# Attention of a graph layer: 24 visits of 53 targets instead of 20 of 63, scores as rows, the mask inside the maximum

## The reference

```python
x = x * rsqrt(mean(x^2) + EPS) * rms_w
x = x @ W_down
xl, xr = (x @ Wl).reshape(n, 4, 64), (x @ Wr).reshape(n, 4, 64)
msg = xl[src] + xr[dst]
act = where(msg > 0, msg, 0.2 * msg)
e = einsum('ehd,hd->eh', act, att)
m = segment_max(e, dst)
p = exp(e - m[dst])
alpha = p / (segment_sum(p, dst)[dst] + 1e-16)
out = segment_sum(alpha[..., None] * xl[src], dst)
out = out.reshape(n, 256) @ W_up
```

## Time and profile before

| | us |
|---|---|
| median of 3 timed runs | 1574.01 (1572.9 to 1575.59) |
| profiled execution: span from first to last instruction | 1688.0 |
| TensorE busy | 1587.7 (94%) |
| VectorE busy | 819.2 (49%) |
| ScalarE busy | 387.0 (23%) |
| GpSimd busy | 259.4 (15%) |
| mean granted TensorE clock | 0.941 of full |

### The profile page before, as it was taken

The page is one execution under the profiler, slowest core; times in us unless marked ns, Lnnn a source line. Parts: engine busy times, 40 slices in busy tenths (PEclk is TensorE's granted clock), DMA queues, the critical chain, the costliest instruction groups (busy, mean ns, idle before and its releaser), DMA issues.

```text
span 1688.0 us, 21080 instructions
## 1 busy us (share of the span) xinstructions
PE 1587.7 (94%) x8256; PEld 1360.5 (81%) x8256; DVE 819.2 (49%) x1262; ACT 387.0 (23%) x699; POOL 259.4 (15%) x306
## 2 busy tenths in 40 slices
...
GB/s 43 177 167 191 128 125 93 129 110 119 137 117 97 112 149 101 115 65 102 132 83 51 127 219 202 88 94 150 0 1 224 187 180 144 156 38 0 63 181 106
DMA packets 99519, 198.38 MB, mean 118 GB/s; under 512 B 24908, under 2 KB 58980, under 8 KB 99420
## 3 DMA queue, kind: packets, MB, share of 16 engines
...
q10 hardware_dynamic: 1482, 0.20, 0.1%
...
## 4 chain that ended last, share of the span: by engine, by line
PE 52%; DVE 1%; ACT 0%; issue 0%; POOL 0%; DVEq 0%; ACTq 0%
PE layers_y_ps L1755 33%; PE layers_y_ps L1776 16%; PE layers_turn_ps L1739 2%; PE layers_up_ps L1723 1%; PE layers_y_ps L1792 1%; DVE layers_w_lo L1912 0%; PE layers_turn_ps L1711 0%; ACT L312 0%; DVE layers_parts_lo L1923 0%; DVE layers_y L1956 0%; POOL out L1696 0%; ACT layers_parts_hi L1867 0%; ACT layers_w_hi L1850 0%; DVE layers_y L631 0%; DVE layers_y L2018 0%
## 5 line engine op out<-in xcount | busy, mean ns | idle before, releaser
L1171 POOL DMA_INDIRECT attention_got<-xl_d,attention_src x130 | 130.5, 1004 | 144.0 <-DVE attention_weighted L1400 101.9
L1213 PEld LDWEIGHTS attention_score_ps<-edges_att_pick,attention_bent 128*128 128x128 f32 x800 | 137.4, 242 | 9.3 <-issue 1.6
L1776 PE MATMUL layers_y_ps<-layers_parts_hi,layers_counts 128*128 128x512 f32 x464 | 143.6, 391 | 0.0
L1776 PE MATMUL layers_y_ps<-layers_parts_lo,layers_counts 128*128 128x512 f32 x464 | 143.3, 390 | 0.0
L1250 PE MATMUL attention_mix_ps<-attention_weighted,attention_hot 128*126 128x260 f32 x400 | 126.9, 439 | 17.0 <-issue 15.5
L1171 POOL DMA_INDIRECT attention_got<-xl_d,heads_first_src x70 | 73.6, 1052 | 353.0 <-issue 308.2
L1755 PE MATMUL layers_y_ps<-layers_w_hi,layers_parts_hi 128*128 128x512 f32 x400 | 125.9, 396 | 0.0
L1755 PE MATMUL layers_y_ps<-layers_w_lo,layers_parts_hi 128*128 128x512 f32 x400 | 123.6, 390 | 0.0
L1755 PE MATMUL layers_y_ps<-layers_w_hi,layers_parts_lo 128*128 128x512 f32 x400 | 123.6, 390 | 0.0
L1213 PE MATMUL attention_score_ps<-edges_att_pick,attention_bent 128*128 128x4 f32 x800 | 121.5, 275 | 1.7 <-issue 1.7
L1360 DVE TENSOR_REDUCE attention_pair_max<-attention_spread_ps 128x2 f32<-128x512 f32 x100 | 68.6, 687 | 95.2 <-PE attention_spread_ps L1219 51.4
(11 more groups left out here) (312 smaller groups left out, 3020.5 us busy)
## 6 DMA issues: line engine op xcount, KB each, us to landing
...
```

The lines of the kernel that those rows point to most:

```text
L1171: pool.indirect_dma_start(got[s][:, t, :], None, xl_d, bass.IndirectOffsetOnAxis(src[s][:, t:t + 1], 0))\
L1213: nc.tensor.matmul(score_ps[j % 2][:, 2 * q + u, :], bent[c][:, k * PAIR + u * P:k * PAIR + (u + 1) * P], g["att_pick"][:, k, :], start=(q ...
L1776: last = nc.tensor.matmul(y_ps[n % 2][:, a:a + HALF], counts[c % 2][:, k, :], part[k][:, a:a + HALF], start=(k == 0 and part is hi), stop= ...
```

## The change

A visit now has 53 targets (24 visits) and a window of 1024 edges, 8 tiles in two quads of 4. The unit of work is 512 edges by one half `k` of the features, four units a visit (`UNITS`), so that a message unit is four transposes and one product of 512 columns. The two copies of the targets now stand on partitions 0 to 52 and 64 to 116 (`PART` = 64).

Scores are now made once, as rows: `att_rows` are the weights, `bent` in f32 is the moving side of 512 columns, and the four units of a visit add up in one PSUM bank `row_ps` (8 rows of 512 edges). ScalarE copies it to fp32r (`take_rows`), and four products (`spread`) by rows of `pick` spread each score over the targets' partitions. The fp32r copy of `bent` and the mask product are gone. The mask is inside the maximum: ScalarE makes `far`, the square of 2^50 times the distance of an edge's target from the partition's node, and VectorE's `take_max` subtracts `far` and takes the maximum with the old best in one operation. From `far` ScalarE also makes `hot_t` by Relu(1 - far / 2^100). VectorE's `find_nodes` is gone. The shift is two products of 512 columns onto `row_ps`; ScalarE copies the result (`take_shifted`), and four transposes (`turn`) put edges back on partitions for clamp and exponential. `mix`, `weigh` and `finish` are as before, on 8 tiles. `clamp`, `exponentials` and `weigh` of visit `j - 2` now stand at `q` = 0 of visit `j`, and the rest of the order is written anew. In `setup` the masks and `att_wide` make way for `pick`, `att_rows` and `far_node`. The rows of `mixed_d` past the last visit are stored by four DMAs instead of one, and fetches of the next stage's rows stand at other visits.

```diff
-SUB = 63
+SUB = 53
 SUBS = -(-NODES // SUB)
-SUB_TILES = 10
+SUB_TILES = 8
 WINDOW = SUB_TILES * P
 GROUP = 32
...
             def messages(i):
-                j, q, b = i // PAIRS_HELD, i % PAIRS_HELD, i % 2
+                j, a, k, b = i // UNITS, i % UNITS // KH, i % KH, i % 2
...
                     pe.wait_ge(bent_ready, i - 1)
-                for u in range(2):
...
+                for t in range(QUAD):
+                    nc.tensor.matmul(message_ps[b][:, t * P:(t + 1) * P], got[s][:, a * QUAD + t, k * P:(k + 1) * P],
+                                     g["ident"][:, :], is_transpose=True, start=(t == 0), stop=False,
+                                     skip_group_check=True)
+                nc.tensor.matmul(message_ps[b][:, :], xr[s][:, k * P:(k + 1) * P],
+                                 hot_t[s][:, a * HALF:(a + 1) * HALF], start=False, stop=True,
+                                 skip_group_check=True).then_inc(message_ready, 1)
...
             def score(i):
-                j, q, b, c = i // PAIRS_HELD, i % PAIRS_HELD, i % 2, i % 3
+                j, a, k = i // UNITS, i % UNITS // KH, i % KH
+                if i % UNITS == 0 and j >= 2:
+                    pe.wait_ge(exp_ready, j - 1)
+                pe.wait_ge(bent_ready, i + 1)
+                nc.tensor.matmul(row_ps[j % 2][:, :], g["att_rows"][:, k, (1 - a) * HEADS:(1 - a) * HEADS + P],
+                                 bent[i % 3][:, :], start=(i % UNITS == 0), stop=(i % UNITS == UNITS - 1),
+                                 skip_group_check=True).then_inc(scored, 1)
+
+            def spread(j, u):
+                i = j * UNITS + u
+                if u == 0:
+                    pe.wait_ge(rows_ready, j + 1)
                 if i >= 2:
                     pe.wait_ge(maxed, i - 1)
-                if q == 0 and j >= 2:
...
+                nc.tensor.matmul(spread_ps[u % 2][:, :], picked(g, 2 * u, 2 * u + 2), score_rows[:, :],
+                                 start=True, stop=True).then_inc(spread_out, 1)
 
             def take_shift(j):
...
-                for t in range(SUB_TILES):
-                    if t == PAIRS_HELD and j >= 1:
-                        mix(j - 1, range(MIX_MID, MIX_END))
...
+                for a in range(QUADS):
+                    last = nc.tensor.matmul(row_ps[j % 2][:, :], shift[j % 2][:, (1 - a) * HEADS:(1 - a) * HEADS + P],
+                                            hot_t[j % 3][:, a * HALF:(a + 1) * HALF], start=False,
+                                            stop=(a == QUADS - 1), skip_group_check=True)
                 last.then_inc(shifted, 1)
...
+
+            def turn(j):
+                pe.wait_ge(shifted_out, j + 1)
+                for t in range(QUAD):
+                    last = nc.tensor.matmul(row_ps[j % 2][:, t * P:(t + 1) * P], shifted_rows[:, t * P:(t + 1) * P],
+                                            g["ident"][:, :], is_transpose=True, start=(t == 0),
+                                            stop=(t == QUAD - 1), skip_group_check=True)
+                last.then_inc(turned, 1)
...
-            for i in range(LAST + PAIRS_HELD + 2):
-                j, q = i // PAIRS_HELD, i % PAIRS_HELD
+            for i in range(LAST + 2 * UNITS):
+                j, q = i // UNITS, i % UNITS
                 if i < LAST:
                     messages(i)
+                if q == 2 and 1 <= j <= SUBS:
+                    spread(j - 1, 0)
+                    spread(j - 1, 1)
+                if q == 3 and 1 <= j <= SUBS:
+                    spread(j - 1, 3)
+                if 2 <= i < LAST + 2:
+                    score(i - 2)
+                if q == 2 and 1 <= j <= SUBS:
+                    spread(j - 1, 2)
+                if q == 1 and j >= 2:
+                    mix(j - 2, range(0, 2))
+                if q == 3 and j >= 2:
+                    mix(j - 2, range(2, 4))
                 if q == 3 and 1 <= j <= SUBS:
                     take_shift(j - 1)
-                if 2 <= i < LAST + 2:
-                    score(i - 2)
-                if q < 2 and 2 <= j <= SUBS:
-                    mix(j - 2, [q])
-                if q == 2 and 2 <= j <= SUBS:
-                    mix(j - 2, range(2, MIX_MID))
-                if q == 0 and j == SUBS + 1:
-                    mix(j - 2, range(SUB_TILES))
+                if q == 3 and j >= 2:
+                    mix(j - 2, range(4, SUB_TILES))
+                if q == 3 and 1 <= j <= SUBS:
+                    turn(j - 1)
                 if j < 2:
-                    fill(4)
+                    fill(8)
...
+            def find_nodes(j):
+                s = j % 3
+                if j >= 1:
+                    act.wait_ge(dst_wide_ready, 16 * j)
+                if j >= 3:
+                    act.wait_ge(maxed, (j - 2) * UNITS)
+                nc.scalar.activation(far[s][:, :].rearrange("p (t e) -> p t e", e=P),
+                                     dst_wide[:, :].rearrange("p (e t) -> p t e", e=P), ACT.Square,
+                                     bias=g["far_node"][:, j:j + 1], scale=BIG_ROOT).then_inc(far_ready, 1)
+                act.wait_ge(far_ready, j + 1)
+                if j >= 3:
+                    act.wait_ge(shifted, j - 2)
+                nc.scalar.activation(hot_t[s][:, :], far[s][:, :], ACT.Relu, bias=g["one"][:, :],
+                                     scale=-1.0 / BIG_ROOT ** 2).then_inc(hot_t_ready, 1)
...
+            def take_rows(j):
+                act.wait_ge(scored, (j + 1) * UNITS)
+                if j >= 1:
+                    act.wait_ge(spread_out, j * UNITS)
+                nc.scalar.activation(score_rows[:, :], row_ps[j % 2][:, :], ACT.Copy).then_inc(rows_ready, 1)
+
...
+            def take_shifted(j):
+                act.wait_ge(shifted, j + 1)
+                if j >= 1:
+                    act.wait_ge(turned, j)
+                nc.scalar.activation(shifted_rows[:, :], row_ps[j % 2][:, :], ACT.Copy).then_inc(shifted_out, 1)
...
-            for i in range(LAST + PAIRS_HELD):
-                j, q = i // PAIRS_HELD, i % PAIRS_HELD
+            find_nodes(0)
+            for i in range(LAST + 2 * UNITS):
+                j, q = i // UNITS, i % UNITS
+                if q == 0 and 2 <= j <= SUBS + 1:
+                    exponentials(j - 2)
                 if i < LAST:
                     scale(i)
-                if q == 3 and j >= 1:
-                    exponentials(j - 1)
-                if i < LAST:
-                    bend(i)
-                if q == 1 and j + 1 in SPLIT_VISITS:
-                    high(SPLIT_VISITS.index(j + 1))
+                if q == 1 and 1 <= j <= SUBS:
+                    take_rows(j - 1)
+                if q == (0 if j == 0 else 2) and j + 1 < SUBS:
+                    find_nodes(j + 1)
+                if q == 3 and 1 <= j <= SUBS:
+                    keep_sums(j - 1)
+                    take_shifted(j - 1)
+                if q == 3 and j in SPLIT_VISITS:
+                    high(SPLIT_VISITS.index(j))
...
+            def take_max(j, u):
+                a, k = u // KH, u % KH
+                dve.wait_ge(spread_out, j * UNITS + u + 1)
+                if u == 0:
+                    dve.wait_ge(far_ready, j + 1)
+                nc.vector.tensor_tensor_reduce(apart[u][:, :], spread_ps[u % 2][:, :],
+                                               far[j % 3][:, a * HALF:(a + 1) * HALF], 1.0, best[:, j, k:k + 1],
+                                               ALU.subtract, ALU.max, unit_max[j % 2][:, a, k:k + 1])\
                     .then_inc(maxed, 1)
 
             def take_best(j):
                 b = j % 2
                 dve.drain()
-                nc.vector.tensor_reduce(new_max[:, :], pair_max[b][:, :, :].rearrange("p q k -> p k q"), AX.X, ALU.max)
-                dve.drain()
-                nc.vector.tensor_tensor(new_best[b][:, :], new_max[:, :], best[:, j, :], ALU.max)
+                nc.vector.tensor_tensor(new_best[b][:, :], unit_max[b][:, 0, :], unit_max[b][:, 1, :], ALU.max)
...
+                nc.vector.tensor_tensor(shift[b][:, HEADS:2 * HEADS].rearrange("p (k t) -> p k t", t=2),
+                                        now.unsqueeze(2).to_broadcast([P, KH, 2]),
+                                        g["part_sign"][:, :].unsqueeze(1).to_broadcast([P, KH, 2]), ALU.mult)\
+                    .then_inc(shift_ready, 1)
+                nc.vector.tensor_tensor(fall[b][:, :], best[:, j, :], now, ALU.subtract).then_inc(fall_ready, 1)
+
+            def keep_best(j):
+                dve.wait_ge(fall_ready, j + 1)
+                nc.vector.tensor_copy(best[:, j, :], new_best[j % 2][:, :].bitcast(F32))
...
+                dve.wait_ge(turned, j + 1)
+                if j >= 1:
+                    dve.wait_ge(exp_ready, j)
+                nc.vector.tensor_scalar(clamped[:, :, :], row_ps[j % 2][:, :].rearrange("p (t r) -> p t r", r=P)
```

(43 more changed lines are left out.)

265 lines of the change are left out of this document (97 added, 168 removed).

## The result

The kernel after takes 1697.6 us (median of 4, 1695.1 to 1698.4) where the kernel before took 1574.8 beside it (4 runs): 1.078 times as long, 95% interval 1.075 to 1.080. The prediction was 1598, its range ended at 1640. The profiled execution is one of the four (1698.3 us, span 1696.6, clock 0.961).

A forecast was written before the change was run, and what follows sets the result against it. TensorE was taken to bound attention before, a dependency ring through three engines after. 24 x 14.35 = 344, plus 6 for splits and 24 for ends, made 374 us of attention against 350: 1574 + 24 = 1598 us, range 1515 to 1640.

The forecast's parts named there:

- The change, part by part: Prediction's section pricing the new attention visit, weight splits, setup, head and tail; attention 374 us against 350.
- The ring: Attention's dependency loop through TensorE, ScalarE and VectorE, expected to set each visit: 14.35 us, 24 visits 344 us.
- my walk: Step-by-step timing of one attention visit, from VectorE's `take_max` of unit 0 to the next: 14.35 us.
- The splits: Five weight splits on VectorE, 1.2 us each, free before and now in the ring: 6 us.
- The ends: Attention's head and tail, kept at 24 us, within 8.
- the 114 us of the profile: Profiled span of the kernel before over its timed median, read as lost in attention to half clock and standstills.
- D: Rival, slower: VectorE's new maximum takes two passes, 35 us more, 1633 us; chance 0.09.
- The Square: ScalarE's Square from strided int32 in attention: 1.04 to 2.1 us, 1.04 taken, ending before the next scale wants the engine.
- C: Rival, slower: the clock falls in attention's new TensorE waits, up to 41 us more, 1639 us; chance 0.14.
- The break-even of 13.3 us a visit: Attention visit length at which the kernel after would equal the kernel before: (350 - 24 - 6) / 24.
- A: Rival, faster: TensorE stays attention's bound at 11.4 us a visit, 1522 us; chance 0.18.
- B: Rival, faster: the 114 us spread evenly, timed runs keeping half clock and standstills, 1490 us; chance 0.11.

The follow-up runs named there:

- e1: Kernel after, with the front stage's loads of targets' own messages and scores cut by partitions, 53 = 48 + 5: 1644.9 us.
- e3: e1 with two more transfers cut 48 + 5, attention's loads of xr and its stores of mixed: 1636.9 us.
- e2: Kernel before, with the front stage's loads of targets' own messages and scores cut by partitions, 63 = 61 + 2: 1749.0 us.
- experiment 1: Kernel before run twice again, nothing changed: 1683.6 us and 1578.4 us.
- e12: e3 with the order on TensorE, VectorE and ScalarE loosened throughout and `keep_sums` behind the exponentials: 1596.2 us, ratio 1.013 to the kernel before.
- e4: e3 with `turn` issued ahead of mix tiles 4 to 7 on TensorE: 1652.1 us.
- e5: e3 with VectorE's `finish` moved from between bend 1 and bend 2 to the end of `q` = 3: 1630.5 us.
- e8: e3 with the running sums left out, `finish` being one small multiplication: 1607.6 us.
- 1660 sessions: Sessions, six of eight, in which the unchanged kernel before had a median of 1654 to 1681 us; in the other two 1575 to 1581.

## Why the prediction was wrong

**The step that failed: "The change, part by part", its list of what is touched.** I costed setup, attention and its head and tail, and nothing in the front stage, though the diff changes SUB and the front stage's loads are shaped by it. Of the 99.6 us missed they are some 58 ahead of attention and 6 in its head, shown from both sides: by cut loads (56 and 6 less in e1 and e3) and by a cut that makes the kernel before 68 us slower (e2). No rival had it. Some 7 us more are setup's clock, which also comes and goes in the kernel before.

**Mis-sized terms of the sum, 35 us together.** I had 344 + 6 + 24 = 374, the stage took 409.
- The ring. 24 x 14.75 = 354 for 344. Each wait is where I put it: TensorE 1.68 ahead of spread 2 and 1.02 ahead of the shift (predicted 2.1 and 0.7), VectorE 2.36 for `clamp` and 1.10 for the first bend (2.2 and 1.1). In a visit of 14.75 the excess over my walk is 0.25 up to bend 3, 0.17 from there to `take_shift` (the maximum is 0.74 for 0.69, and a read of its accumulator of 0.08 stands behind it) and 0.18 to the first bend; 0.2 comes back behind it, `finish` being 1.8 for 1.98.
- The splits: 1.9 to 2.3 us each, 10 for 6.
- The ends: 409 - 354 - 10 = 45 us for 24. Before, they are 25. Most of it is the head: from the stage's start to the first weighing it takes 50 us after and 35 before. Of these 15 us 6 are the front stage's loads again. The other 9 were not taken apart; the first weighing now stands behind two whole visits of messages and stood behind 1.7 before, and that lag I named and gave nothing.

**What held.** That the 114 us of the profile lie in attention (experiment 1), and so 350 us of attention: 347. TensorE busy in 80% of the stage (327 of 409). No table load behind the stage's start. The maximum at 0.74, within its bounds and one pass, so D falls. The Square was 2.14 us, the upper bound, and off the ring as I had it. C happened only in small: the clock falls for 3.4 us seven times from 420 to 780, and visits without a split stay at 14.75 to 15.1. The break-even of 13.3 us a visit was too kind, since it rests on 24 us for the ends: e12's visits have a mean of 13.55 from the first weighing to the last, which with the splits in it is the break-even (13.3 + 6/24), yet e12 is 1.3%, 21 us, behind the kernel before.

**The rivals.** A: TensorE is not the bound. I wrote that 1 us off my walk would gain; e4, e5 and e8 show that 1 or 2 us off single steps give at most 0.35 to 0.7 us a visit, and e4 a loss, as other chains lie within a microsecond. B: refuted by the layers' constant 906 us, but its premise, that timed runs can keep the half clock, is true in 1660 sessions; there the kernel after is 3% slower than the kernel before (1.030), not 8%.

Open: what makes a session one or the other. One chip (13) had the kernel before at 1581 in one session and at 1654 in another, so it isn't the chip alone. Not tried: the kernel after with attention as before and SUB at 54 or 56.
